# TensorE's opening and its wide chunks in four branches that the first of two turns hops over (adjacency product with layer norm, float32)

## The reference

```
def _L0_gnn_ref(x, adj, u):
    P_DROP = 0.1
    keep = (u >= P_DROP).astype(x.dtype)
    x_drop = x * keep / (1.0 - P_DROP)
    return jnp.matmul(adj, x_drop)
x = _layernorm(x + _L0_gnn_ref(x, adj, L0_gnn_u), axis=-1)
```

## Time and profile before

| | us |
|---|---|
| median of 3 runs (641.74 to 641.94) | 641.75 |
| the profiled execution | 641.88 |
| its span | 640.1 |
| TensorE busy with matmuls | 502.8 |
| VectorE busy | 53.7 |
| ScalarE busy | 17.7 |
| DMA, mean over the span | 429 GB/s |

### The profile page before, as it was taken

How to read it: one execution, slowest core, us unless ns; L and a number is a source line. 1 busy time by engine, 2 the same in 40 slices (tenths; PEclk the granted TensorE clock), 3 DMA queues, 4 the chain that set the end, 5 groups by cost and what they waited for, 6 DMA issues and landing times.

```text
span 640.1 us, 5097 instructions
## 1 busy us (share of the span) xinstructions
PE 502.8 (79%) x2312; PEld 179.7 (28%) x2312; DVE 53.7 (8%) x102; ACT 17.7 (3%) x41; POOL 1.6 (0%) x14
## 2 busy tenths in 40 slices
PE   0097969688799578879878689867869868689997
PEld 0062213232233222223222223222323223133344
DVE  1930001010010100101000010100101001010101
ACT  0001000000000000000000000000000000000000
POOL 1000000000000000000000000000000000000000
PEclk9997979988799978889979899978999969799999
DMA  9999999999999999999999999999999999999998
GB/s 393 459 394 455 431 420 454 405 446 439 422 421 436 435 451 422 438 408 444 459 418 434 442 412 455 420 434 446 426 418 426 446 451 422 438 405 438 425 425 364
DMA packets 7207, 274.84 MB, mean 429 GB/s; under 512 B 800, under 2 KB 928, under 8 KB 1312
## 3 DMA queue, kind: packets, MB, share of 16 engines
q1 hardware_dynamic: 7056, 272.63, 98.8%
q10 hardware_dynamic: 144, 2.10, 0.8%
HBM read 272.63 MB, written 2.10 MB: 429 GB/s over the span
## 4 chain that ended last, share of the span: by engine, by line
DMA 62%; PE 33%; DVE 3%; another core or an unknown queue 1%; issue 0%; ACT 0%; SPq 0%; DVEq 0%; ACTq 0%
DMA ring<-adj 56%; PE acc L202 33%; DMA ring<-adj_last 5%; DMA xdrop<-u 2%; DVE node_sum L317 1%; DVE xdrop L321 1%; DVE xdrop L329 1%; PE folded L210 0%; DVE x_sb L321 0%; PE lifted L237 0%; SPq L126 0%; ACT squares L303 0%; PE lifted L263 0%; ACT std L308 0%
## 5 line engine op out<-in xcount | busy, mean ns | idle before, releaser
L202 PE MATMUL acc<-ring,xdrop 128*64 128x512 f32 (+1 forms) x2176 | 485.6, 606 | 103.1 <-DMA ring<-adj 101.7
L202 PEld LDWEIGHTS acc<-ring,xdrop 128*64 128x64 f32 x2176 | 162.8, 146 | 413.0 <-issue 280.2
L344 DVE SCALAR_TENSOR_TENSOR y<-folded,x_sb 128x256 f32<-128x256 f32 (+1 forms) x16 | 6.7, 416 | 552.3 <-PE folded L210 552.3
L237 PE MATMUL lifted<-x_sb,lift 128*128 128x64 f32 x4 | 1.1, 428 | 30.6 <-DVE x_sb L321 30.6
L210 PEld LDWEIGHTS folded<-fold,sums_T 128*128 128x128 f32 x128 | 15.5, 191 | 12.6 <-issue 12.6
L284 ACT COPY sums_T<-acc 128x512 f32<-128x512 f32 x15 | 8.8, 585 | 335.0 <-PE acc L202 335.0
L210 PE MATMUL folded<-fold,sums_T 128*128 128x64 f32 x128 | 17.7, 281 | 0.0
L277 ACT ACTIVATE std<-square_sum,eps 128x4 f32<-128x4 f32 (+1 forms) x16 | 4.8, 297 | 225.2 <-DVE square_sum L351 225.2
L237 PEld LDWEIGHTS lifted<-x_sb,lift 128*128 128x128 f32 x4 | 0.9, 322 | 30.5 <-issue 30.5
L348 DVE TENSOR_TENSOR squares<-y 128x256 f32<-128x256 f32 (+1 forms) x16 | 6.7, 417 | 0.5
L355 DVE TENSOR_TENSOR x_sb<-y,rstd 128x256 f32 (+1 forms) x16 | 6.7, 416 | 0.6
(11 more groups left out here) (23 smaller groups left out, 5.5 us busy)
## 6 DMA issues: line engine op xcount, KB each, us to landing
ring<-adj SPq DMA_DIRECT2D x13, 4096.0 KB, 31.3
ring<-adj SPq DMA_DIRECT2D x2, 2048.0 KB, 28.7
xdrop<-u ACTq DMA_DIRECT2D x1, 2048.0 KB, 12.5
x_sb<-x SPq DMA_DIRECT2D x1, 2048.0 KB, 12.3
out<-x_sb SPq DMA_DIRECT2D x1, 1984.0 KB, 12.7
ring<-adj_last SPq DMA_DIRECT2D x1, 1920.0 KB, 29.5
ring<-adj_last SPq DMA_DIRECT2D x1, 1792.0 KB, 33.4
ring<-adj_last SPq DMA_DIRECT2D x1, 1536.0 KB, 30.6
```

Source lines behind the costliest of these rows:

```text
L202: last = nc.tensor.matmul(acc[i][D * h:D * h + D, 0:cols], xdrop[:, k, :], piece[:, b, :], start=(k < 2), stop=(k >= NB - 2))
L344: nc.vector.scalar_tensor_tensor(out=y[:, 0:nj, :], in0=folded[:, 0:nj, :], scalar=1.0 / KEEP, in1=x_sb[:, bass.ds(block0, nj), :], op0=AL ...
```

## The change

TensorE's program gets an outer loop of two turns. The opening, which was straight code, and the five wide chunks of the inner loop's body stand in branches that are entered in the second turn alone: one for the opening and three in the loop's body, for chunks 0 and 1, chunks 2 and 3, and chunk 4 of each five. In the first turn TensorE hops over all of them: once over the opening, and three times over the three stretches. The products, their operands, the waits on data and the signals are those of before, in the same order; the other engines' instructions aren't touched. `half`, `products` and `fold_rows` are unchanged.

```
+STRETCHES = ((0, 1), (2, 3), (4,))
...
-            pe.wait_ge(lift_ready, 1)
-            pe.wait_ge(x_centred, 1)
...
-            with pe.Fori(0, (CHUNKS - 1) // RING) as f:
-                for v, i in enumerate(ACC_OF):
-                    for n in range(HALVES):
-                        half(i, f, v * HALVES + n)
-                        if n == 0:
-                            fold_rows(f * RING + v)
+            def opening():
+
+                pe.wait_ge(lift_ready, 1)
+                pe.wait_ge(x_centred, 1)
+                for j in range(LAST_J):
+                    nc.tensor.matmul(lifted[:, j, 0:D], lift[:, :], x_sb[:, NB - LAST_J + j, :],
+                                     start=True, stop=False)
+                pe.wait_ge(fold_ready, 1)
+
+                pe.wait_ge(row_in[0], 16)
+                for n in range(HALVES):
+                    pe.wait_ge(dropped, n + 1)
+                    first = first_narrow + n * HALF
+                    last = products(1, narrow[:, first:first + HALF, :], n * HALF, HALF, LAST_COLS)
+                    if n % 2:
+                        last.then_inc(half_used, 1)
+
+            def wide_chunk(f, v):
+                for n in range(HALVES):
+                    half(ACC_OF[v], f, v * HALVES + n)
+                    if n == 0:
+                        fold_rows(f * RING + v)
+
+
+            with pe.Fori(0, 2) as turn:
+                with pe.If(turn > 0):
+                    opening()
+
+                with pe.Fori(0, (CHUNKS - 1) // RING) as f:
+                    for stretch in STRETCHES:
+                        with pe.If(turn > 0):
+                            for v in stretch:
+                                wide_chunk(f, v)
```

## The result

The changed kernel takes 643.22 us (median of 14 runs, 642.78 to 643.36), the one before, on the same chips, 641.77 (14 runs, 641.65 to 642.08). The ratio is 1.0021, 95% interval 1.0014 to 1.0029: **slower by 1.45 us**, where the forecast was 0.4 us faster and the range ended at 642.1. The profiled execution of the change, 642.78, is its fastest run, with a span of 641.0.

A forecast was written before the change was run, and what follows sets the result against it. Adjacency arriving through the 16 DMA engines was taken as the bound. First turn and branches cost 0; lateness of 1.40 us less 1.0 for a loaded fetch gave 0.4 us off 641.75, so 641.35 us, range 640.3 to 642.1.

The forecast's parts named there:

- What bounds the kernel: Whole run: adjacency coming in over 16 DMA engines sets the time, 19.365 us a row; the slowest engine delays every landing.
- The first turn, cost 0: TensorE's start: hops and three missed lines at some 2 us each end by about 10 us, ahead of 30.57; cost 0.
- The branches of the second turn, cost 0: Second turn: ten entries and ten jumps, 3.2 us in the sequencer, hidden under 24 waits of 4.2 us; cost 0.
- The lateness of the engines: Early fetches beside x and u: each loaded one costs its engine 0.60 to 1.40 us, taken as 1.0; gain 0.4 us.
- One loaded fetch keeps the whole price: Early fetches: only the worst engine counts, so the gain is 1.40 us less one loaded fetch's cost, 0 to 0.8.
- rival 2: Early fetches: all the lateness goes, requests going out in the first 2 us or hitting engines that start first; 640.35 us, chance 0.12.
- Rival 3: TensorE's instruction memory: hops drive lines out, over 30 packets, deciding beyond 16 when an engine is hit twice; 643.2 us, chance 0.05.
- Rival 1: Line fetches: the lateness stays whole, late fetches under load costing as much as at 46 us; 641.75 us, chance 0.27.

The follow-up runs named there:

- e8: The changed kernel with five stretches of one chunk, so each hop lands in the very next line: 642.46 us, in two groups of runs.
- e2: The changed kernel with TensorE waiting for x and u to land before its first turn: 645.33 us.
- e1: The changed kernel without its first turn, all branches kept: 641.86 us, ratio 1.0000 to the kernel before.
- r1: The changed kernel as it is, measured once more: 643.23 us.
- e6: The changed kernel with one stretch of all five chunks, so the first turn makes one far hop over them: 643.51 us, ratio 1.0027.
- f4: The changed kernel with the two turns around the opening alone and the loop outside them: 641.85 us, ratio 0.9999.
- e9: e8 with row 2's load issued as two halves, the first at once: 641.90 us, ratio 1.0002.
- e3: The changed kernel with SyncE's and ScalarE's first loads held until TensorE's first turn is through: 658.47 us.
- f1: e3 without 48 of the 64 products of the last half chunk, all loads kept: 658.83 us.

## Why the prediction was wrong

- *What bounds the kernel*: right. The stream of adjacency keeps 19.367 us a row, and the time is set by the slowest of 16 engines. The nine engines in front finish alike in both kernels.
- *The first turn, cost 0*: right on the path, but mis-sized. Three missed lines took 6.1 to 7.2 us each instead of 2, and the turn ended at 25.3, not 10. The cover held by 5 us; in e8 and e2 it didn't. (1,920 instructions over seven lines are 274 a line, not 250; the targets of the hops were counted with 256, and six lines came early, as it said.)
- *The branches of the second turn, cost 0*: right (e1: 641.86).
- *The lateness of the engines*: **the step that failed**. "At most the 1.40 that it costs now" was no bound. That number came from fetches that came singly, 29 us or more apart; the text itself had a hop ask for "one or two more at the same time, nearly free", and its rest go one by one. In the two profiles of the change the second fetch of a pair took 1.5 to 2.1 us instead of 1.0, both engines of a pair were left late, and the worst ended 2.4 and 3.0 us behind the nine instead of 1.4. The sentence "a gain is excluded only below 0" shut out the side on which the result lay. Of the forecast's 0.4 us nothing came; the term was +1.45, of which r1 shows 1.41 in the landings.
- *One loaded fetch keeps the whole price*: right, and it holds for the seventh. That packet stood in the earlier trace rows, at 624 to 641 us, ahead of the last landings, and rival 2 (and the sentence that with no fetch loaded the gain is all 1.40) overlooked it: with all six lines free the time would have been about 0.2 under before, not 1.40.
- *Rival 3* named 643.2 and slower, but by lines driven out and over 16 packets. There are seven, so its number is right by chance. The part on an engine hit twice is real, but it is e6 that shows it, at the ninth packet, and e6 alone brings lines twice. The window of two pages of "Runtime: NRT & Kernel Launch" in the Trainium skill, section Instruction fetch mechanics, on which it leaned, isn't what TensorE shows here: before, three passes over six lines brought each once.
- *Rival 1*, the lateness stays whole, is what f4 and e9 do (641.85 and 641.90), but not the change.

## What to carry to other kernels

When a kernel is bound by DMA, a line of program is a transfer too: it makes one of the 16 engines late for as long as the queue stays full, here to the end of the run, and only the worst engine counts, so moving fetches earlier gains nothing unless the engines are idle and no fetch is left, not even one near the end. If lines are asked for ahead, ask for them one by one, and keep their number small: seven fell on seven engines in every profile, and in the one run with nine an engine was hit twice. And a bound taken from a row holds only for the pattern of that row: things that came apart in the trace of before may cost more together.

## What the runs showed that was not expected

- A hop into a line that isn't there takes 5.0 to 9.3 us under load (change, e2, e8, e9) and 3.1 to 5.0 us with the DMA engines idle (e3, f1), although the packet itself takes 1 to 2.5. What fills the rest no record shows.
- Why two fetches close together cost more, idle engines or not (e3: 6.4% of 16 times 3 us in 2:5, 3.1 us for two), is open too. They go to different engines, so it isn't that one engine carries both. Nor does a packet's length tell its price: the change's fetch at 4.49 took 0.93 us and had ended when the next began, yet four engines are 1.79 us late or more; the same fetch alone, in f4, leaves 1.21.
- TensorE's memory kept the six lines of a loop of 1,370 instructions over three passes (no packet from 215 to 624 us), and in the change's turn 1 all of what turn 0 had brought. In e6, whose first turn went over the whole body in one hop, it didn't keep all of it.
- A branch taken to a line that is there costs the sequencer 0.21 to 0.25 us (0.37 for the first hop, over the opening), one not taken 0.07 to 0.08.
